# A WKV recurrence and a mixture of experts, one sequence apart, unrolled into one stage

## The chip, the cores and the metric

The kernel runs on one core of one Trainium2 chip. The metric is device microseconds, lower is better: the median of three runs, each of which is one execution of the whole program.

## The reference

Two blocks work on x, four sequences of 1024 tokens with 128 channels, f32. The first block (attention over whole sequences and six layers of local attention with feed-forward parts) is not touched. The second block is:

```python
h = _layernorm(x) * (1 + ca) + sa
x = x + ga * wkv(h)              # recurrence along each sequence
h = _layernorm(x) * (1 + cb) + sb
x = x + gb * mixture(h)          # per token, two of eight experts
# wkv:
r, v, k = split(h @ W_rvk.T)
#   per step: p = max(pp, u + k_t); e1 = exp(pp - p); e2 = exp(u + k_t - p)
#             y = (e1*aa + e2*v_t) / (e1*bb + e2)
#             p2 = max(pp + w, k_t); aa, bb, pp updated with exp(pp + w - p2), exp(k_t - p2)
out = (sigmoid(r) * y) @ W_out.T
# mixture:
probs = softmax(h @ gate_w.T); top2_w, top2_idx = top_k(probs, 2)
expert_out = silu(einsum(h, expert_w) + expert_b)      # all eight
out = sum(expert_out[top2_idx] * top2_w) @ combine_w.T
```

The recurrence needs its whole sequence in order, the mixture only its own tokens. So the mixture of sequence b needs the recurrence of sequence b and nothing of a later one.

## The kernel before

x stays in SBUF, transposed: 128 channels on the partitions, 4096 tokens along them. The program is a row of stages, each a block with its own instruction stream for every engine: `prepare`, `theta_attention`, `local_layers`, then `rwkv` and `mixture`. Between blocks all engines meet. Inside a block each engine has a queue that runs strictly in the order in which it is written, and waits on semaphores that other engines raise.

`rwkv` takes one sequence (1024 tokens) a step. TensorE makes k, v and r in three PSUM tiles of two banks each; ScalarE copies k and v, takes tanh of r (sr). VectorE makes pp, the running maximum, with a scan, then the arguments e1, e2, f1, f2 of four exponentials, which ScalarE takes. The denominators bb and the numerators aa are two more scans; then come den, its reciprocal, num, the output projection and the residual. GpSimd makes e2v and f2v. `step(n, late)` runs the recurrence of sequence `late` and puts the two layer norms of the next sequence n behind the arguments. A layer norm goes from engine to engine: mean on TensorE, centring on VectorE, squares on ScalarE, variances on TensorE, eleven small VectorE operations for 1/sqrt, a transpose that spreads it, the product on VectorE, the output on ScalarE.

`mixture` takes half a sequence (a chunk of 512 tokens) a step; there are eight. For each expert e TensorE multiplies (`ps_e`), ScalarE applies silu (`y`), GpSimd widens the gate (`wide`), TensorE transposes it (`ps_g`), VectorE multiplies both (`yg`, the function `gated`) and TensorE adds the product into the combined sum (`ps_c`). The layer norm, softmax and choice of the two best for the next chunk stand between the eight gatings. GpSimd widens one expert ahead. A chunk that is done is stored by the sync engine. exp and silu need different tables on ScalarE, so a switch between them has an ACT_TABLE_LOAD.

## Time and profile before

| | |
|---|---|
| Median of the three runs | 5023.8 us (5016.67 to 5025.26) |
| Profiled execution, its own time | 5043.72 us |
| Its span, first to last instruction | 5041.9 us |
| Mean granted TensorE clock | 0.945 |
| Recurrence stage, from 4588 us of the span | 234.0 us |
| Mixture stage, to the end of the span | 220.0 us |

The profile is of one execution. An engine's busy time is the time in which it executes; its waits are idle time in front of an instruction, put down to what ended them. The granted clock is 1.00 at TensorE's full speed (2.4 GHz) and 0.50 at half (1.2 GHz). In names from the profile, wkv_ stands for tiles of `rwkv` and moe_ for tiles of `mixture`. In a row of windows the busy times stand in the order TensorE matmul, TensorE weight load, VectorE, ScalarE, GpSimd, each with its number of instructions; then the clock, the DMA share and GB/s. An f32 matmul leaves two records.

### The profile page before, as it was taken

To read this page: it belongs to the slowest core of one execution; us is meant where nothing else is said; L and a number is where in the kernel's file an instruction comes from. 1 tells how busy PE (TensorE), PEld (TensorE's weight loads), DVE (VectorE), ACT (ScalarE), POOL (GpSimd) and SP (SyncE) were. 2 spreads that over 40 slices of the span, in tenths; PEclk is the share of its full clock that TensorE was granted. 3 is DMA by queue.
4 is the path that set the end of the run, shared out by engine and by line. 5 is a ranking of instruction groups with operands and counts; after the bars stand their busy time and mean duration, and the time that the engine had idled before them with its cause. 6 is when DMAs were issued, how large, how long until landed. Compare 5 with 4: busy or idle time off the path is not lost. (4 is left out here: it accounts for less than half of the span.)

```text
span 5041.9 us, 174816 instructions
## 1 busy us (share of the span) xinstructions
PE 4035.4 (80%) x68188; PEld 2875.6 (57%) x68188; DVE 3716.5 (74%) x6687; ACT 3142.5 (62%) x8425; POOL 1080.8 (21%) x856
## 2 busy tenths in 40 slices
PE   7948888888888888888888888888888888884358
PEld 4625665666666666666656665565666665652134
DVE  4837777777777777777777777777787787765655
ACT  4716666666776676776666666666666667661123
POOL 0002222222222222222222222222222222210011
PEclk9959999999999999999999999999999999996679
DMA  0012222222222222222222222222222222220000
GB/s 26 1 57 86 73 77 71 83 86 75 78 73 75 89 85 75 75 75 82 86 76 70 77 73 85 81 79 73 76 74 90 77 77 73 73 65 3 0 9 13
DMA packets 126159, 336.66 MB, mean 67 GB/s; under 512 B 32592, under 2 KB 33744, under 8 KB 125264
## 3 DMA queue, kind: packets, MB, share of 16 engines
q1 hardware_dynamic: 125520, 326.63, 20.1%
q8 instruction: 586, 9.60, 0.9%
q14 instruction: 53, 0.43, 0.0%
HBM read 22.41 MB, written 2.10 MB: 5 GB/s over the span
## 5 line engine op out<-in xcount | busy, mean ns | idle before, releaser
L1172 ACT ACTIVATE loc_probs<-loc_pair,loc_ebias,loc_rnorm 128x64 f32<-128x64 f32 x3072 | 1200.4, 432 | 11.6 <-DVE loc_ebias L1332 8.4
L873 POOL TENSOR_TENSOR loc_ks<-loc_mcos,loc_swapped 128x1024 f32<-128x1024 f32 x192 | 451.9, 2354 | 1771.7 <-DVE loc_kr L1320 1378.2
L920 PE MATMUL loc_pair<-loc_hs,loc_wqk 128*128 128x256 f32 x3072 | 750.8, 388 | 49.6 <-issue 45.3
L873 POOL TENSOR_TENSOR loc_qr<-loc_mcos,loc_swapped 128x1024 f32<-128x1024 f32 x192 | 452.1, 2355 | 1283.2 <-DMA loc_swapped<-loc_msin 1207.1
L1172 ACT ACTIVATION_READ_ACCUMULATOR loc_probs<-loc_pair,loc_ebias,loc_rnorm 128x1 f32 x3072 | 717.2, 233 | 0.0
L920 PEld LDWEIGHTS loc_pair<-loc_hs,loc_wqk 128*128 128x128 f32 x3072 | 568.3, 192 | 153.9 <-issue 66.3
L1330 DVE TENSOR_REDUCE loc_mx<-loc_pair 128x8 f32<-128x512 f32 x384 | 264.6, 689 | 413.7 <-PE loc_pair L964 399.0
L1272 DVE SCALAR_TENSOR_TENSOR loc_mcos<-loc_pair,loc_scal,loc_tab 128x1024 f32<-128x1024 f32 x384 | 490.5, 1277 | 85.1 <-ACT loc_sq L1154 66.7
L1154 ACT ACTIVATE loc_sq<-loc_pair 128x1024 f32<-128x1024 f32 x384 | 396.7, 1033 | 207.0 <-PE loc_pair L920 207.0
L1281 DVE SCALAR_TENSOR_TENSOR loc_msin<-loc_pair,loc_scal,loc_tab 128x1024 f32<-128x1024 f32 x384 | 489.7, 1275 | 9.1 <-DMA loc_swapped<-loc_msin 8.5
L964 PE MATMUL loc_pair<-loc_kr,loc_qr 64*32 64x64 f32 x24576 | 320.7, 225 | 126.7 <-issue 126.1
L977 PE MATMUL loc_pair<-loc_wv,loc_hs 128*64 128x512 f32 x1536 | 410.2, 659 | 1.6 <-DVE loc_o L1348 1.4
L1183 ACT ACTIVATE loc_vodd<-loc_pair 128x1024 f32<-128x1024 f32 x192 | 196.8, 1025 | 338.6 <-DMA loc_veven<-loc_vodd 206.0
L964 PEld LDWEIGHTS loc_pair<-loc_kr,loc_qr 64*32 64x32 f32 x24576 | 271.9, 105 | 226.8 <-issue 224.7
L1001 PE MATMUL loc_pair<-loc_veven,loc_probsT 64*32 64x64 f32 x12288 | 308.9, 226 | 84.9 <-issue 83.7
L1332 DVE SCALAR_TENSOR_TENSOR loc_ebias<-loc_mx,loc_rnorm 128x8 f32<-128x8 f32 x384 | 366.2, 954 | 13.2
L1190 ACT ACTIVATE loc_probsT<-loc_pair 128x1024 f32<-128x1024 f32 x192 | 195.8, 1020 | 275.9 <-PE loc_pair L986 275.9
L1197 ACT ACTIVATE loc_oT<-loc_pair 128x1024 f32<-128x1024 f32 x192 | 194.9, 1015 | 264.6 <-PE loc_pair L1011 264.6
L1021 PE MATMUL loc_one<-loc_oT,loc_wo 128*128 128x256 f32 x1536 | 347.6, 380 | 0.8 <-DVE loc_act_out L1393 0.4
L1001 PEld LDWEIGHTS loc_pair<-loc_veven,loc_probsT 64*32 64x32 f32 x12288 | 261.0, 105 | 148.5 <-issue 147.8
L1054 PE MATMUL loc_one<-loc_h,loc_w 128*128 128x256 f32 (+1 forms) x1152 | 322.6, 404 | 19.3 <-ACT loc_h L1211 8.1
L1001 PE MATMUL loc_pair<-loc_vodd,loc_probsT 64*32 64x64 f32 x12288 | 315.1, 227 | 5.0 <-issue 5.0
(240 smaller groups left out, 7440.5 us busy)
## 6 DMA issues: line engine op xcount, KB each, us to landing
loc_swapped<-loc_msin SPq DMA_DIRECT2D x768, 256.0 KB, 2.6
loc_veven<-loc_vodd SPq DMA_DIRECT2D x768, 64.0 KB
loc_veven<-loc_vodd SPq DMA_DIRECT2D x384, 128.0 KB
loc_wqk<-wqk_dram SPq DMA_DIRECT2D x12, 512.0 KB, 4.7
loc_wv<-wv_dram SPq DMA_DIRECT2D x6, 512.0 KB, 4.4
loc_wo<-wo_dram SPq DMA_DIRECT2D x6, 512.0 KB, 4.4
x<-xT_dram SPq DMA_DIRECT2D x1, 2048.0 KB, 7.3
loc_tab<-tables_dram SPq DMA_DIRECT2D x1, 2048.0 KB, 7.5
```

What stands on the lines that cost most here:

```text
L873: nc.gpsimd.tensor_tensor(dst, mcos[i % 2][:, :], swapped[:, :], ALU.add).then_inc(rope_add, 1)
L920: ins = nc.tensor.matmul(pairs[b][:, p // 2, (p % 2) * UNIT:(p % 2 + 1) * UNIT], wqk[:, k, w:w + P], hs[u.odd][:, :], start=True, stop=True)
L964: ins = nc.tensor.matmul(pairs[b][WIN * w:WIN * w + WIN, hp, p * 2 * WIN:(p + 1) * 2 * WIN], qr[u.odd][part, p, at:at + WIN], kr[u.odd][pa ...
L977: ins = nc.tensor.matmul(pairs[b][hp * DH:(hp + 1) * DH, g, :], hs[u.odd][:, BLK * x + DH * g:BLK * x + DH * g + DH], wv[:, hp, :], start= ...
L1001: ins = nc.tensor.matmul(pairs[b][WIN * w:WIN * w + WIN, hp, p * DH:(p + 1) * DH], probsT[part, p, WIN * w:WIN * w + WIN], v[part, w // 2, ...
L1021: ins = nc.tensor.matmul(bank(b)[:, 0:UNIT], wo[:, p, :], oT[:, p, :], start=p == 0, stop=p == PAIRS - 1)
L1054: ins = nc.tensor.matmul(bank(b)[0:FB[j], k * UNIT:(k + 1) * UNIT], w1[:, at:at + FB[j]], h[:, :], start=True, stop=True)
L1154: nc.scalar.activation(sq[:, i, :], flat(b), ACT.Square).then_inc(sq_ready, 1)
L1172: ins = nc.scalar.activation(probs[x][:, p, hp, :], pairs[b][:, hp, p * 2 * WIN:(p + 1) * 2 * WIN], ACT.Exp, bias=ebias[x][:, k:k + 1], sc ...
L1272: nc.vector.scalar_tensor_tensor(mcos[i % 2][:, :].rearrange("p (g t) -> p g t", g=4), flat(b).rearrange("p (g t) -> p g t", g=4), scal[u. ...
L1281: nc.vector.scalar_tensor_tensor(msin[:, :].rearrange("p (g t) -> p g t", g=4), flat(b).rearrange("p (g t) -> p g t", g=4), scal[u.odd][:, ...
L1332: nc.vector.scalar_tensor_tensor(ebias[x][:, k], mx[x][:, k], -1.0, rnorm[u.odd][:, x, HEADS:].rearrange("p (g y) -> p y g", y=2)[:, hp, : ...
```

## The change

`rwkv` and `mixture` become one block, `recurrence_and_mixture`, without loops. It is written out as stages: for each sequence b two halves (`part` 0 and 1). The first has the recurrence of b from the projections to the scan of the denominators, the second from the scan of the numerators to the residual, and the layer norms of sequence b+1. Beside them stand the eight experts of chunk `late` = n-1, and the norm and the choice of experts of chunk n = 2(b-1)+part. So the recurrence of sequence 0 has no mixture beside it, that of sequence 1 has chunk 0 in its second half, those of 2 and 3 have a chunk in each half, and three chunks are left after them.

To fit both into eight PSUM banks the recurrence has one bank (`ps_w`) for all projections: six matmuls of 512 tokens, each after ScalarE has emptied the bank, and an output projection in two halves, each after the other's residual. All layer norms share one set of buffers. The squares of a chunk's norm, before on VectorE, are taken on ScalarE. The weights of both parts are loaded at the start, and the first mean does not wait for them.

```diff
-def rwkv(nc, const, t):
+def recurrence_and_mixture(nc, const, t, out):
...
+        def both(stage):
+            for b in range(BATCH + 1):
+                for part in range(2):
+                    n = 2 * (b - 1) + part
+                    stage(part, b if b < BATCH else None, b + 1 if b + 1 < BATCH else None, n if n >= 0 else None, n - 1 if n >= 1 else None)
+            stage(0, None, None, None, NCH - 1)
...
+            def project(b, i):
+                if b is None:
+                    return
+                which, c = (2, 1, 0)[i // 2], i % 2
+                if i == 0:
+                    if b == 0:
+                        pe.wait_ge(wkv_loaded, START + 32)
+                    pe.wait_ge(ln.out_ready, START + norm_of_sequence(b, 1) + 1)
+                    pe.wait_ge(xw_done, START + 2 * b)
+                pe.wait_ge(proj_ready, START + 6 * b + i)
+                nc.tensor.matmul(ps_w[:, :], w[:, which, :], wh[:, half(c)], start=True, stop=True).then_inc(proj_ps, 1)
+            def project_out(b, c):
+                if b is None:
+                    return
+                pe.wait_ge(wy_ready, START + b + 1)
+                pe.wait_ge(proj_ready, START + 6 * b + 6)
+                pe.wait_ge(xw_done, START + 2 * b + c)
+                nc.tensor.matmul(ps_w[:, :], w[:, 3, :], num[:, half(c)], start=True, stop=True).then_inc(wout_ps, 1)
...
+                if part == 1:
+                    project_out(b, 0)
+                expert(late, 5)
+                combine(late, 4)
+                if part == 0:
+                    project(b, 5)
+                else:
+                    project_out(b, 1)
+                    if after_b is not None:
+                        mean(norm_of_sequence(after_b, 0), slice(after_b * SEQ, after_b * SEQ + CH))
+                expert(late, 6)
...
+            def times_values(b, i):
+                if b is None:
+                    return
+                pool.wait_ge(proj_ready, START + 6 * b + 4)
+                own_wait(pool, passed)
+                pool.wait_ge(wexp_ready, START + 4 * b + 2 * i + 2)
+                own_wait(pool, passed)
+                dst, src = ((e2v, e2), (f2v, f2))[i]
+                nc.gpsimd.tensor_tensor(dst[:, :], src[:, :], v[:, :], ALU.mult).then_inc(den_part, 1)
+            def stage(part, b, after_b, n, late):
+                for e in range(EXPERTS):
+                    widen(late, e)
+                    if part == 0 and e == 4:
+                        times_values(b, 0)
+                if part == 0:
+                    times_values(b, 1)
+            both(stage)
...
+            def stage(part, b, after_b, n, late):
                 if n is not None:
-
+                    if n == 0:
+                        act.wait_ge(moe_loaded, START + 80)
+                    ln.scalar_squares(act, norm_of_chunk(n))
+                silu(late, 0)
+                if part == 0:
+                    project_out(b, 0)
+                silu(late, 1)
+                if part == 0:
+                    project_out(b, 1)
+                if n is not None:
                     act.wait_ge(mods_ready, START + n + 1)
-                    for c in range(2):
-                        ln.scalar_squares(act, n * 2 + c)
-                        ln.scalar_out(act, n * 2 + c, [(slice(0, P), h[:, c * CH:(c + 1) * CH])], mods[:, 0:1])
-
-            sequences(act, step)
+                    ln.scalar_out(act, norm_of_chunk(n), [(slice(0, P), h[:, n % 2, :])], mods[:, n % 2, 0:1])
+                silu(late, 2)
+                if part == 0:
+                    project_out(b, 2)
+                silu(late, 3)
+                if part == 0:
+                    project_out(b, 3)
+                if n is not None:
+                    act.wait_ge(centred, START + n + 1)
+                    nc.scalar.activation(probs[:, :, :], logits[:, :, :], ACT.Exp).then_inc(exp_ready, 1)
+                if part == 0:
+                    exponential(b, 0)
+                    exponential(b, 1)
+                silu(late, 4)
+                silu(late, 5)
+                if part == 0:
+                    project_out(b, 4)
+                    project_out(b, 5)
+                    exponential(b, 2)
+                    exponential(b, 3)
+                elif after_b is not None:
+                    ln.scalar_squares(act, norm_of_sequence(after_b, 0))
+                silu(late, 6)
+                silu(late, 7)
+                if part == 1 and after_b is not None:
+                    sequence_out(after_b, 0)
+                    ln.scalar_squares(act, norm_of_sequence(after_b, 1))
+                    sequence_out(after_b, 1)
...
+            def first_part(b, n, late):
+                chunk_mods(n)
+                gated(late, 0)
+                if n is not None:
+                    rstd(norm_of_chunk(n))
+                gated(late, 1)
+                largest(b)
+                if n is not None:
+                    normed(norm_of_chunk(n), mods[:, n % 2, 1:2])
+                gated(late, 2)
+                arguments_state(b)
+                centred_logits(n)
+                gated(late, 3)
+                larger_now(b)
+                gated(late, 4)
+                arguments_now(b, 0)
+                softmax(n)
+                gated(late, 5)
+                arguments_now(b, 1)
+                two_best(n)
+                gated(late, 6)
+                denominators(b)
+                gated(late, 7)
+                chunk_done(late)
+            def second_part(b, after_b, n, late):
+                chunk_mods(n)
+                numerators(b)
+                gated(late, 0)
+                if n is not None:
+                    rstd(norm_of_chunk(n))
+                gated(late, 1)
+                denominators_now(b)
+                if n is not None:
+                    normed(norm_of_chunk(n), mods[:, n % 2, 1:2])
+                gated(late, 2)
+                reciprocals(b)
+                centred_logits(n)
+                gated(late, 3)
+                numerators_now(b)
+                received(b)
+                gated(late, 4)
+                softmax(n)
+                gated(late, 5)
+                if after_b is not None:
+                    sequence_mods(after_b)
+                residual(b, 0)
+                residual(b, 1)
+                if after_b is not None:
+                    centre(norm_of_sequence(after_b, 0), slice(after_b * SEQ, after_b * SEQ + CH))
+                two_best(n)
+                gated(late, 6)
+                if after_b is not None:
+                    rstd(norm_of_sequence(after_b, 0))
+                gated(late, 7)
+                if after_b is not None:
+                    normed(norm_of_sequence(after_b, 0), wmods[:, 1:2])
+                chunk_done(late)
+                if after_b is not None:
+                    sequence_norm(after_b, 1)
...
@@ -1808,9 +1996,7 @@
         if phases >= 2:
             local_layers(nc, const, t)
         if phases >= 3:
-            rwkv(nc, const, t)
-        if phases >= 4:
-            mixture(nc, const, t, out)
+            recurrence_and_mixture(nc, const, t, out)
         else:
             store(nc, const, out)
```

VectorE, in the second half of a recurrence, before (loop written out once for the last sequence): bb and aa are the scans, then den, its reciprocal and num.

```order
L1588 SCALAR_TENSOR_TENSOR wkv_bb<-wkv_e 128x1024
L1590 SCALAR_TENSOR_TENSOR wkv_aa<-wkv_e,wkv_e2v 128x1024
L1593 TENSOR_TENSOR wkv_den<-wkv_f,wkv_bb 128x1024
L1594 TENSOR_TENSOR wkv_den<-wkv_den,wkv_f 128x1024
L1595 RECIPROCAL wkv_den<-wkv_den 128x1024
L1596 TENSOR_TENSOR wkv_num<-wkv_f,wkv_aa 128x1024
L1598 TENSOR_TENSOR wkv_num<-wkv_num,wkv_f2v 128x1024
L1599 TENSOR_TENSOR wkv_num<-wkv_num,wkv_den 128x1024
```

The same place now, in a stage with a chunk beside it (tail_ names all tiles of the new block; yg is the gating of an expert; one and logits belong to the next chunk):

```order
L1767 TENSOR_TENSOR tail_yg<-tail_y,tail_ps_g 128x512
L1819 RECIPROCAL tail_den<-tail_den 128x1024
L1860 TENSOR_REDUCE tail_one<-tail_ps_small 128x4
L1861 TENSOR_TENSOR tail_logits<-tail_ps_small,tail_one 128x32
L1767 TENSOR_TENSOR tail_yg<-tail_y,tail_ps_g 128x512
L1824 TENSOR_TENSOR tail_num<-tail_f,tail_aa 128x1024
L1826 TENSOR_TENSOR tail_num<-tail_num,tail_f2v 128x1024
L1831 TENSOR_TENSOR tail_num<-tail_num,tail_den 128x1024
L1833 SCALAR_TENSOR_TENSOR tail_num<-tail_sr,tail_num 128x1024
L1767 TENSOR_TENSOR tail_yg<-tail_y,tail_ps_g 128x512
```

Between two gatings there is now the reciprocal and the centring of the logits, and between the next two all four products that end in num.

ScalarE, in the first half of a recurrence, before: the copy of v, tanh and four exponentials in one row.

```order
L1536 ACTIVATE wkv_v<-wkv_ps 128x1024
L1539 ACTIVATE wkv_sr<-wkv_ps 128x1024
L1542 ACTIVATE wkv_e<-wkv_e 128x1024 x2
L1542 ACTIVATE wkv_f<-wkv_f 128x1024 x2
```

The same place now (y0 and y1 are silu outputs of experts 3, 4 and 5; probs is the exponential for the gates):

```order
L1692 ACTIVATE tail_y<-tail_ps_e1,tail_expert_b 128x512
L1674 ACTIVATE tail_v<-tail_ps_w 128x512
L1722 ACT_TABLE_LOAD
L1722 ACTIVATE tail_probs<-tail_logits 128x32
L1684 ACTIVATE tail_e1<-tail_e1 128x1024
L1684 ACTIVATE tail_e2<-tail_e2 128x1024
L1692 ACT_TABLE_LOAD
L1692 ACTIVATE tail_y<-tail_ps_e0,tail_expert_b 128x512
L1692 ACTIVATE tail_y<-tail_ps_e1,tail_expert_b 128x512
L1677 ACTIVATE tail_sr<-tail_ps_w 128x512 x2
L1684 ACT_TABLE_LOAD
L1684 ACTIVATE tail_f1<-tail_f1 128x1024
```

The two silus of experts 4 and 5 stand behind three exponentials and two table loads, and tanh, which has no load of its own behind silu, stands behind them.

## Rows read from the trace of the kernel before

**Rows 1.** The page, part 1: busy us, share of the span, instructions.
```profile
PE 4035.4 (80%) x68188; PEld 2875.6 (57%) x68188; DVE 3716.5 (74%) x6687; ACT 3142.5 (62%) x8425; POOL 1080.8 (21%) x856
```

**Rows 2.** Windows, both stages: from:to, length, busy us by engine, clock, DMA.
```profile
4588.00:4822.00 234.00, 78.04 (x176) 38.96 (x176) 149.58 (x181) 40.07 (x46) 20.23 (x8) 0.57 0.00 1
4822.00:5042.00 220.00, 183.81 (x688) 100.44 (x688) 111.61 (x384) 72.62 (x97) 39.02 (x64) 0.91 0.04 13
```

**Rows 3.** Waits in the recurrence stage: total us, times, longest.
```profile
PE wkv_ps L1508 <- DVE wkv_num L1602: 88.5, 4, 28.9
...
DVE wkv_ln_var L194 <- PE wkv_ps_small L168: 21.0, 8, 2.7
...
PE wkv_ps_ln L162 <- DMA wkv_decay<-wkv_decay_dram: 16.3, 1, 16.3
```

**Rows 4.** Waits in the mixture stage.
```profile
DVE moe_yg L1737 <- ACT moe_y L1717: 49.3, 30, 2.9
```

**Rows 5.** Windows, one recurrence step: arguments, norms ahead, scans to num, output.
```profile
4669.30:4682.80 13.50, 6.25 (x14) 2.58 (x14) 10.49 (x7) 6.23 (x6) 2.34 (x1) 0.85 0.00 0
4682.80:4700.80 18.00, 8.04 (x26) 5.50 (x26) 6.84 (x30) 3.15 (x6) 2.35 (x1) 0.50 0.00 0
4700.80:4720.00 19.20, 0.23 (x1) 0.23 (x2) 18.28 (x9) 0.63 (x1) 0.00 (x0) 0.50 0.00 0
4720.00:4725.30 5.30, 3.71 (x5) 1.24 (x6) 1.44 (x2) 0.00 (x0) 0.00 (x0) 0.71 0.00 0
```

**Rows 6.** Windows, one mixture chunk beside the next one's norm; the last chunk.
```profile
4897.40:4922.00 24.60, 21.80 (x88) 11.86 (x87) 14.20 (x48) 8.90 (x12) 4.85 (x8) 1.00 0.03 11
5020.80:5038.60 17.80, 17.55 (x64) 8.81 (x63) 6.27 (x10) 5.50 (x8) 3.68 (x6) 1.00 0.04 15
```

**Rows 7.** Groups by line, VectorE in the recurrence stage: count, busy us, mean ns, idle before.
```profile
L1595 DVE RECIPROCAL wkv_den<-wkv_den 128x1024 f32<-128x1024 f32 x4 | 26.2, 6553 | 0.1
...
L1599 DVE TENSOR_TENSOR wkv_num<-wkv_num,wkv_den 128x1024 f32<-128x1024 f32 x4 | 4.9, 1226 | 0.1
```

**Rows 8.** Timeline, recurrence stage: start us, us, engine, line, idle before.
```profile
4591.44 2.08 PE L162 MATMUL wkv_ps_ln<-x,mean_w 128*128 128x512 f32 x2 [16.31 <-DMA wkv_decay<-wkv_decay_dram]
...
4596.92 0.16 DVE L194 TENSOR_SCALAR wkv_ln_var<-wkv_ps_small 128x4 f32<-128x4 f32 x1 [2.68 <-PE wkv_ps_small L168]
4597.12 0.17 DVE L91 TENSOR_SCALAR wkv_ln_rstd<-wkv_ln_var 128x4 int32<-128x4 int32 x1
...
4601.13 2.07 PE L162 MATMUL wkv_ps_ln<-x,mean_w 128*128 128x512 f32 x2 [0.84 <-DVE wkv_ln_normed L202]
...
4611.51 8.25 PE L1500 MATMUL wkv_ps<-wkv_h,wkv_w 128*128 128x512 f32 x12 [1.59 <-ACT wkv_h L222]
...
4669.34 5.39 PE L1500 MATMUL wkv_ps<-wkv_h,wkv_w 128*128 128x512 f32 x12 [1.59 <-DVE x L1605]
...
4676.04 2.19 ACT L1542 ACTIVATE wkv_e<-wkv_e 128x1024 f32<-128x1024 f32 x2 [0.24 <-DVE wkv_e L1570]
```

**Rows 9.** Timeline in a mixture chunk: ScalarE's table loads, exp and silu.
```profile
4910.25 1.28 ACT L1723 ACT_TABLE_LOAD   x1
...
4911.54 0.23 ACT L1723 ACTIVATE moe_probs<-moe_logits 128x32 f32<-128x32 f32 x1
4911.79 1.28 ACT L1717 ACT_TABLE_LOAD   x1
...
4913.09 1.46 ACT L1717 ACTIVATE moe_y<-moe_ps_e,moe_expert_b 128x512 f32<-128x512 f32 x2
```

**Rows 10.** Timeline, GpSimd's product e2v and VectorE's f1.
```profile
4678.31 2.34 POOL L1522 TENSOR_TENSOR wkv_e2v<-wkv_e,wkv_v 128x1024 f32<-128x1024 f32 x1 [47.91 <-ACT wkv_e L1542]
4678.37 3.35 DVE L1574 TENSOR_TENSOR wkv_f<-wkv_pp,wkv_pm 128x1024 f32<-128x1024 f32 x1
```

**Rows 11.** Windows of 1 us, as matmuls end and 3 us later.
```profile
4620.00:4621.00 1.00, 0.62 (x2) 0.00 (x0) 1.00 (x1) 1.00 (x2) 0.00 (x0) 1.00 0.00 0
4624.00:4625.00 1.00, 0.00 (x0) 0.00 (x0) 1.00 (x1) 0.68 (x1) 1.00 (x1) 0.54 0.00 0
```

More of the change, by code:

```diff
@@ L1693, in _ @@
+            for c in range(2):
+                ln.tensor(pe, c, x[:, half(c)], ps_ln[:, :], ps_small[:, 0:4])
+            both(stage)
         @block.gpsimd
         def _(pool):
[L1695 to L1703 removed]
@@ L1797, in kernel_program @@
+            sequence_mods(0)
+            for c in range(2):
+                sequence_norm(0, c)
+            dve.wait_ge(w_ready, START + 1)
+            link(nc.vector.tensor_scalar(wdec[:, :], ew[:, :], -1.0, None, ALU.mult))
+            dve.wait_ge(init, START + 1)
+            dve.wait_ge(wkv_loaded, START + 32)
+            dve.wait_ge(moe_loaded, START + 80)
+            both(stage)
 def kernel_program(nc, t, out, phases=5):
```

553 lines of the change are left out of this document (287 added, 266 removed).

## The prediction

> **What bounds the kernel now.** I read the page first: over the whole span TensorE is busy 80% and VectorE 74% [rows 1], but that is mostly the long local-attention part, which the change leaves alone. So I cut out the two stages that it touches. The recurrence stage is 234.0 us and the mixture stage 220.0 us, 454.0 together, a tenth of the span [rows 2]. In the first VectorE works 149.6 us, TensorE 78.0 at a mean granted clock of 0.57; in the second TensorE works 183.8 and VectorE 111.6 [rows 2]. So one is led by VectorE, the other by TensorE, and each leaves the other engine free for half its time: VectorE work adds up to 261.2 us of the 454.
>
> The chain of waits says how each is bound. In the recurrence TensorE waits 88.5 us for the last product num, and VectorE waits 21.0 for the variances [rows 3]: a serial chain. In the mixture VectorE waits 49.3 us for y [rows 4], while TensorE idles little. One recurrence step in windows [rows 5]: projections and arguments 13.5, the two layer norms of the sequence ahead 18.0 with VectorE at 6.8, scans to num 19.2 with VectorE at 18.3, output projection and residual 5.3. A mixture chunk is 24.6 us with VectorE at 14.2; the last one, with no chunk behind it, 17.8 [rows 6].
>
> **The change.** It removes no arithmetic. It puts the mixture of sequence b-1 into the VectorE, ScalarE, GpSimd and TensorE queues between the pieces of the recurrence of sequence b. What it adds: two more table loads; projections one bank at a time; residual in two halves (0.2 us a sequence). The squares of a mixture chunk move from VectorE (0.9) to ScalarE. Every queue runs in order, so the new time is VectorE's work plus the waits that its order leaves. I go through it by sequence.
>
> *Opening.* Before, the first mean starts at 4591.4, behind the weight transfers (TensorE's wait of 16.3 ends there), and the first projection at 4611.5, so 23.5 us from 4588 [rows 3, 8]. Now mean and centring start without that wait and only ScalarE's squares still need it: about 3 less, 20.5.
>
> *Sequence 0* has no mixture beside it. Arguments: 13.5 with half of its matmuls at the high clock [rows 5]; these are cold and go through one bank, each waiting for ScalarE's copy of the one before, so 17. Then 19.2 from the first scan to num [rows 5], of which the reciprocal is 6.55 [rows 7] (18.3 less it and less six products of 1.23 leaves 2.2 to 2.3 for each of the two scans); output in two halves, each waiting for the other's residual, 5.5; then the norms of sequence 1: 8.7 partly begun under the residual, and 9.6 (4601.13 less 4591.44 is 9.7 [rows 8]) with nothing beside it. In all 60, against 57.8 before (4611.5 to 4669.3 [rows 8]).
>
> *Sequence 2, the full case.* VectorE's work: recurrence 10.5 - 2.1 (a stall told below) + 18.3 + 1.4 + 0.2 = 28.3; norms of the next sequence 6.8 [rows 5]; two chunks of 14.2 less 0.9 for the squares, 26.6 [rows 6]. That is 61.7. Some 100 small operations follow each other 0.20 apart though each lasts 0.16 or 0.17 (4596.92, 4597.12 [rows 8]): 4 more, 65.7. Waits, walked in queue order with TensorE at 2.15 an expert (17.8 / 8 [rows 6]), silu 0.7, table load 1.28 [rows 9]:
> - centring waits for the mean in both halves, 1.3; the first gating for a silu behind the squares, 1.4; the variances, 0.5; the third gating of each half for a silu that now stands behind the norm's output on ScalarE, 2 x 1.45.
> - the fifth gating of the first half: on ScalarE its silu is behind load, exp of the gates, two exps of 1024 columns (2.19 for a pair [rows 8]), load: 1.28 + 0.23 + 2.2 + 1.28 + 0.7 = 5.7 after the v copies, where VectorE has only 1.8 of work: 3.8. The seventh gating behind tanh, load, two exps, load: 1.0.
> - end of chunk 0.5; residual of the second half 0.9; second norm of the next sequence, exposed behind the last gating, 3.2.
>
> Waits 15.5, so 81. To this I add 4 for the clock: TensorE stands still under the reciprocal and the products behind it, and a stretch without matmuls lets the clock fall (1.00 in 4620 to 4621 as the matmuls end, 0.54 in 4624 to 4625 [rows 11]); what is cold then is one output projection, two experts and the mean. And 3 for the port, below. 88.
>
> *Sequence 1* is without the eight gatings in its first half: 72 + 3 + 2 = 77. *Sequence 3* is without the next norms and their wait: 72 + 4 + 3 = 79. *After the last recurrence* two chunks as now, 49.2, and the last with the store, 17.8 + 3.2 = 21.0.
>
> Sum: 20.5 + 60 + 77 + 88 + 79 + 49 + 21 = 394.5, against 454: **60 us less**. The profiled execution took 5043.7 us for its span of 5041.9; the median of the runs is 5023.8, 20 below it. The part that differs is the same in both, so I take 60 off the median: 4964.
>
> **The port.** While GpSimd's product e2v runs from 4678.31 for 2.34, VectorE's f1, begun at 4678.37, takes 3.35 where a 1024-column product alone takes 1.23 [rows 7, 10]. It stood still for 2.1, until GpSimd was done. The new stage has 40 gate copies of 0.61 on GpSimd beside sequences 1 to 3, where they used to run beside gatings that read PSUM. If each costs VectorE nothing it is 0; if each hits a product of SBUF operands at its start, 40 x 0.6 = 24. Most copies start as TensorE ends a transpose, at random against VectorE, which is in such products a third of the time: I take 8.
> The Trainium skill, "SBUF — State Buffer", section "Who interferes with whom", says that a VectorE instruction with two SBUF inputs and a GpSimd instruction that reads SBUF exclude each other for the whole of the one begun first. By that, the trace agrees, and the loss to VectorE is capped at the copy's own length.
>
> **Table loads.** From 4910.25 a load of 1.28, exp at 4911.54, the next load at 4911.79, silu at 4913.09 [rows 9]: a switch costs 1.28 and no more. The Trainium skill, "ScalarE: Activation LUTs", section "What ACT_TABLE_LOAD costs", has about 2.66 us for a switch, drain included. By it the fifth and seventh gating of sequences 2 and 3 would come 4 to 5 later each time and the sum would be about 9 higher, 4973. The row decides here.
>
> **The rivals.**
> - *Nothing but VectorE's work counts* in sequences 1 to 3. For: VectorE's pieces are long enough to cover most round trips. Against: the waits above are by order, not by speed. Work is 66 + 59 + 58 = 183 against 244, 61 more, so 4903 at the bound; half of it, 4934. Chance 8%.
> - *TensorE stays at the low clock* through sequences 1 to 3. For: the recurrence stage has 0.57 [rows 2] and the gaps in it stay. Against: the mixture stage has 0.91, and chunks put work on TensorE every 3 us. Its work in sequence 2 is two chunks of 21.8 [rows 6], eight projections of 0.9 (six take 5.39 [rows 8]) and two norms of 2 (8.0 at the low clock, [rows 5]), 54.8 at the high clock and 109 at the low: 21 over my 88, 30 with a few waits kept. Sequence 3 is two chunks and the projections, 50.8 and 101, 22 over; sequence 1, with one chunk, 73, 0 to 8 over. In all 43 to 60 more, 5014 in the middle. Chance 9%.
> - *The queues lock*: every in-order engine waits at another's piece, and a stage is the sum of its parts: 56 + 49 for sequence 2 (17 over), 15 over for each other, so 47 and 5011. For: ScalarE's queue now has both chains. Chance 6%.
> - *Slower, by the port.* If a copy that meets a scan of 2.3 us waits for it, TensorE's transposes wait for the copy, and the gating for them, each of the 40 costs the 2.1 that the product in [rows 10] lost: 84 us, 5048. It decides from 1.5 us a copy (60 / 40). Against: the copies run one expert ahead. Chance 4%.
>
> **The numbers.** My forecast has 73%. The own range of the forecast: waits and adders 15 off either way, 4949 to 4979. To leave out no more than 2 in 10 I reach to the half-way case below and into the cold-clock case above: 4938 to 5006. A measurement of this kernel tells 0.2%, 10 us, from no change (the three runs spread over 8.6). Faster by more: the forecast, the first rival, half of the second and of the third (below 5014), 0.89. Within: the other halves, 0.07. Slower: 0.04.
>
> **What would show it.** In the changed profile the combined stage lasts 380 to 410 us; VectorE is busy 250 to 270 us of it; sequence 2 takes 82 to 94 us and is the longest. The longest wait of VectorE on ScalarE stands before the fifth gating (the line of yg), 3 to 5 us, twice. The reciprocal has mixture work of TensorE and ScalarE under it. Granted clock 0.8 to 0.95 in sequences 2 and 3, 0.5 in sequence 0. The local layers are unchanged. Wrong would be: a clock near 0.5 beside the mixture, products of VectorE with a mean far above 1.5 us, or gatings that wait 2 us nearly every time.

## The result, and the profile after

The changed kernel took 4974.65 us in the median of four runs (4962.77 to 4999.60), the kernel before 5024.53 beside it. The ratio is 0.9906, 95% interval 0.9881 to 0.9930. A second set of five runs gave 4972.76 and 0.9896 (0.9878 to 0.9915). The forecast was 4964.

Single runs of one kernel lie up to 43 us apart (5009.73 to 5052.84 for the kernel before, in the last set), so the profiles are compared by their **tail**: the time from the end of VectorE's last update of x in the local layers, which the change leaves alone, to the end of the span. That update in the kernel before (timeline; start, duration, eight instructions):

```profile
4576.19 10.35 DVE L1444 SCALAR_TENSOR_TENSOR x<-loc_xa,mod,x 64x1024 f32<-64x1024 f32 x8
```

It ends at 4586.54, and the span at 5041.9: a tail of 455.4. The same row and the span in the changed kernel:

```profile
4569.25 10.34 DVE L1444 SCALAR_TENSOR_TENSOR x<-loc_xa,mod,x 64x1024 f32<-64x1024 f32 x8
```

```profile
core 0: 4983.1 us, clock 0.950
```

It ends at 4579.59, so the tail is 403.5, **51.9 us shorter**. The other 6.9 of the 58.8 between the two spans lie in the untouched layers. Over all kernels measured here their end varies from 4551 to 4592. The page's part 1, to set against [rows 1]:

```profile
PE 4053.0 (81%) x68188; PEld 2876.0 (58%) x68188; DVE 3701.7 (74%) x6683; ACT 3147.4 (63%) x8447; POOL 1095.9 (22%) x856
```

The shares hardly move, since the tail is a twelfth of the span. Windows by sequence of the new stage (columns as in [rows 2]). The second begins at the first projection, the later ones where VectorE starts on the next stage's factors of the norm:

```profile
4579.90:4602.90 23.00, 10.14 (x29) 6.05 (x29) 6.89 (x30) 4.05 (x6) 0.14 (x3) 0.50 0.15 39
4602.90:4662.60 59.70, 25.44 (x44) 9.29 (x44) 38.80 (x45) 9.34 (x13) 7.33 (x2) 0.53 0.00 0
4662.60:4741.90 79.30, 55.63 (x152) 27.98 (x152) 57.18 (x132) 22.12 (x31) 14.27 (x12) 0.69 0.01 4
4741.90:4834.30 92.40, 66.83 (x216) 34.34 (x216) 61.24 (x142) 31.26 (x42) 19.55 (x18) 0.83 0.02 6
4834.30:4915.90 81.60, 63.65 (x191) 31.67 (x192) 54.13 (x113) 29.39 (x39) 19.57 (x18) 0.83 0.01 4
4915.90:4983.10 67.20, 60.03 (x235) 31.88 (x233) 32.30 (x103) 24.34 (x34) 13.38 (x22) 0.99 0.05 17
```

These are the opening, sequences 0 to 3, and the chunks left over. VectorE is busy 250.5 us of 403. Sequence 2 is the longest, and there VectorE works 61.2 of 92.4. The clock rises from 0.53 with no mixture beside the recurrence to 0.83 with a chunk in each half. What VectorE waits for in the tail (total us, times, longest):

```profile
DVE tail_yg L1767 <- ACT tail_y L1692: 56.3, 32, 4.6
DVE tail_ln_var L194 <- PE tail_ps_small L168: 20.7, 10, 5.1
```

The wait for num that held TensorE for 88.5 us [rows 3] has shrunk to 31.3, of which 20.9 are one wait, that of sequence 0. The dearest wait of VectorE is the one for y, 56.3 us, where it was 49.3 in the mixture alone [rows 4]. Groups by line in the tail:

```profile
L1637 POOL COPY tail_wide<-tail_gates 128x512 f32<-128x512 f32 x64 | 51.4, 813 | 189.7 <-PE tail_ps_g L1550 189.7
...
L1819 DVE RECIPROCAL tail_den<-tail_den 128x1024 f32<-128x1024 f32 x4 | 26.2, 6546 | 0.0
...
L1801 DVE TENSOR_TENSOR_SCAN tail_bb<-tail_e 128x1024 f32<-128x1024 f32 x4 | 11.9, 2974 | 0.1
```

GpSimd's gate copies have a mean of 813 ns, where a copy alone takes 610. The reciprocal is unchanged from [rows 7]. The scan bb has a mean of 2974 ns where a scan alone takes 2290.

### The profile page after: what moved, and what is told of

Its sections match the earlier page's. It is cut to its first block and busy times, and to the rows that moved or that the text cites. A ratio compares the mean times of both kernels' runs of the same rounds, so it can differ in the third digit from the quotient of the medians.

```text
span 4983.1 us, 174228 instructions
## 1 busy us (share of the span) xinstructions
PE 4053.0 (81%) x68188; PEld 2876.0 (58%) x68188; DVE 3701.7 (74%) x6683; ACT 3147.4 (63%) x8447; POOL 1095.9 (22%) x856
## 3 DMA queue, kind: packets, MB, share of 16 engines
q1 hardware_dynamic: 125520, 326.63, 20.4%
## 5 line engine op out<-in xcount | busy, mean ns | idle before, releaser
L1332 DVE SCALAR_TENSOR_TENSOR loc_ebias<-loc_mx,loc_rnorm 128x8 f32<-128x8 f32 x384 | 379.8, 989 | 13.2
```

What stands on the lines that cost most here:

```text
L1332: nc.vector.scalar_tensor_tensor(ebias[x][:, k], mx[x][:, k], -1.0, rnorm[u.odd][:, x, HEADS:].rearrange("p (g y) -> p y g", y=2)[:, hp, : ...
```

## The experiments

Each kernel differs from the changed one by the edit shown; the code is cut. e4_narrow_copy and e11_narrow_values also set their tiles to zero once, and e1_serial numbers the layer norms in its own order. e2, e3, e4 and e11 leave out or replace part of the computation; the others compute all of it. A time is one run where no number stands beside it, and each tail is read from one profile.

| kernel | its time, us | tail, us | to 403.5 |
|---|---|---|---|
| changed, second set | 4972.76 (5 runs) | 404.2 | +0.7 |
| e1_serial | 5029.79 | 451.9 | +48.4 |
| e2_one_table | 4955.29 | 393.4 | -10.1 |
| e3_short_recip | 4931.85 | 378.6 | -24.9 |
| e4_narrow_copy | 4955.33 | 399.1 | -4.4 |
| e5_silu_first | 4979.24 | 398.1 | -5.4 |
| e6_regroup | 4986.88 | 393.0 | -10.5 |
| e7_filler | 4974.95 | 399.4 | -4.1 |
| e8_split_reciprocal | 4987.67 | 404.0 | +0.4 |
| e9_all_three | 4958.69 (6 runs) | 384.1 | -19.4 |
| e11_narrow_values | 4964.37 | 387.0 | -16.5 |
| e12_values_on_vector | 4955.74 (5 runs) | 387.1 | -16.4 |

**How far a tail can be trusted.** The changed kernel once more, unedited.

> The changed kernel once more, unedited, for more runs of it beside those of the kernel before and of the version with three edits. Its tail should be 403.5 within 1 us while its whole time differs from the first profile's by up to 30 us, if what varies between runs lies in the local layers ahead of the tail. Rival: the tail varies as well, by some 3 us or more, and then differences of 4 us in the other runs mean nothing.

Its profile has a span 12.2 us shorter and a tail 0.7 us longer. So what varies lies mostly ahead of the tail, and a difference of 4 us between tails is read here as one of the kernels. The 0.7 lies in sequence 0 (60.6 for 59.8); sequences 1 to 3 and the chunks left agree within 0.1 us in the two profiles (79.3, 92.3, 81.7 and 67.1). All this rests on two profiles of the same kernel.

**Merging without overlap.**

```diff
-            for b in range(BATCH + 1):
+            for b in range(BATCH):
                 for part in range(2):
-                    n = 2 * (b - 1) + part
-                    stage(part, b if b < BATCH else None, ...)
+                    stage(part, b, b + 1 if b + 1 < BATCH else None, None, None)
+            for n in range(NCH):
+                stage(n % 2, None, None, n, n - 1 if n >= 1 else None)
```

> The same single unrolled block, but all four recurrences first and the eight chunks after them, nothing side by side. I read the tail: from the end of VectorE's last update of x in the local layers to the end of the span (455.4 us before, 403.5 in the changed kernel). My theory, that the overlap is the gain: about 450 (the pause of 7.6 us between the two blocks goes and the opening is 1.5 shorter; one bank for the projections gives some 3 back in a sequence). Rival, that one block without loops and branches is itself the gain: 405 to 425.

The tail is 451.9, 3.5 under the kernel before. Of the 51.9 us, 48.4 come from the overlap and 3.5 from everything else that the rewriting did. VectorE's largest wait in this kernel (total us, times, longest):

```profile
DVE tail_yg L1768 <- ACT tail_y L1693: 60.9, 43, 2.9
```

The wait for y is 60.9 us without overlap and 56.3 with it. The overlap hides mixture work inside the recurrence; it does not shorten the mixture's own round trip.

**Table loads.**

```diff
-nc.scalar.activation(y[...], ps_e[...], ACT.Silu, bias=...)
+nc.scalar.activation(y[...], ps_e[...], ACT.Tanh, bias=...)
```

> silu of the experts is replaced by tanh, which stands in one table with exp, so that no table is loaded in the stage after the first (part of the computation is changed). Tail 403.5 in the changed kernel. My theory, that the fifth and seventh gating wait for silus behind two table loads each: about 386, with the waits before these gatings down from 4.6 and 3.9 us to 2 or less each. Rival, that VectorE's work hides the loads: 400 or more.

Nineteen loads of 1.28 us are gone, 24.4 us of ScalarE, and the tail is 10.1 shorter, a little over half of what the theory had. Sequence 1 keeps its 79.3; the gain is 4.2 in sequence 2, 3.5 in sequence 3 and 2.3 in the chunks left. The longest wait for y is now 2.1:

```profile
DVE tail_yg L1767 <- ACT tail_y L1692: 39.0, 29, 2.1
```

In sequence 2 the fifth gating waits 1.79 and the seventh 1.95, where they waited 4.64 and 3.92. So a load counts only where a gating waits for it: of the 24.4 us, 10.1 came out of the tail. The Trainium skill, "ScalarE: Activation LUTs", section "What ACT_TABLE_LOAD costs", has 1283 ns for the load and some 1380 more for a drain; the first part agrees with the rows, the second is not seen: in the timeline of sequence 2 below, a load of 1.28 begins at 4775.78 and silu at 4777.07.

**Is VectorE's queue the bound?**

```diff
-link(nc.vector.reciprocal(den[:, :], den[:, :]))
+link(nc.vector.tensor_tensor(den[:, :], den[:, :], f2[:, :], ALU.mult))
```

> The reciprocal of den (6.55 us) is replaced by a product with f2 (1.23 us), which changes part of the computation. Tail 403.5 in the changed kernel; in the kernel before the same edit could give at most 4 x 5.3 = 21. My theory, that VectorE's queue sets the time but experts run under the reciprocal: all of 5.3 in sequence 0 and 3.5 in each of the others, so about 387. Rival, that TensorE or ScalarE set the time beside the mixture: 5 to 8 in all, 396 or more.

VectorE has 4 x 5.33 = 21.3 us less work, and the tail is 24.9 shorter, where the theory had some 16: the whole of the work came out, and 3.6 besides. By sequence the gain is 5.7, 8.2, 6.9 and 4.0. Sequence 2 of this kernel takes 85.4, 7 less than the 92.4 above for 5.3 less work, at a clock of 0.86, where it was 0.83 (in sequence 1 0.79, where it was 0.69):

```profile
4699.70:4785.10 85.40, 64.49 (x216) 33.59 (x216) 56.24 (x142) 31.25 (x42) 20.10 (x18) 0.86 0.02 7
```

That the higher clock gives the 3.6 would fit, but no run shows it.

Cutting the same reciprocal in two halves, with a gating between them:

```diff
-                reciprocals(b)
+                reciprocals(b, 0)
                 centred_logits(n)
                 gated(late, 3)
+                reciprocals(b, 1)
```

> The reciprocal of 1024 columns (6.54 us) is made in two halves of 512, and the centring of the logits and the fourth gating stand between the halves instead of behind both. The full computation is made. Tail of the changed kernel: 403.5 us. Theory: what the reciprocal costs is its time on VectorE, and VectorE's queue sets the end, so an order alone gives back no more than TensorE's idle time under it is worth: tail 401 to 406. Rival: the single block of 6.5 us hurts by its length, since TensorE, ScalarE and GpSimd run dry and the clock falls; cut in two it costs 2 to 3 us less in each of sequences 1 to 3: tail 394 to 398.

The tail is 404.0. It is the time on VectorE that costs, not the length of the block.

**GpSimd's gate copies.**

```diff
-nc.gpsimd.tensor_copy(wide[:, e % 2, :, :], bcast_last(gates[...], P))
+nc.gpsimd.tensor_copy(wide[:, e % 2, :, 0:8], bcast_last(gates[...], 8))
```

> GpSimd widens each gate to 8 columns instead of 128 (the rest of the tile stays zero, so part of the work is left out); its 64 copies are much shorter. Tail 403.5 in the changed kernel. My theory, that the shared port costs little through these copies: 400 to 403. Rival, that the copies block VectorE's products beside the mixture: 385 to 395.

4.4 us for 64 copies whose time on GpSimd falls from 51.4 to 20.4, a little more than the theory's 0.5 to 3.5; 3.6 of it is in sequences 1 to 3, the rest in the chunks left. What the remaining 20.4 us of copies cost no run shows. That settles the rival "slower, by the port": it needed 1.5 us a copy.

**GpSimd's products with the values.**

```diff
-nc.gpsimd.tensor_tensor(dst[:, :], src[:, :], v[:, :], ALU.mult)
+nc.gpsimd.tensor_tensor(dst[:, 0:8], src[:, 0:8], v[:, 0:8], ALU.mult)
```

> GpSimd's two products with the values are made on the first 8 of their 1024 columns, the rest is zero, so the recurrence's numerator is changed. Tail of the changed kernel: 403.5 us. Theory: VectorE's scan bb and product den of sequence 0 (4.44 and 3.18 us, where other sequences show 2.29 and 1.22) and its f2 and scan aa of sequence 1 (3.31 and 3.15, where others show 1.28 and 2.29) are longer because GpSimd's product runs beside them; they fall to the short values, 7 us less: tail 395 to 398. Rival: they are long for another reason, or the time goes into waits: tail 402 to 404.

16.5 us, over twice what was expected. The four places named did fall to their short values, and VectorE's busy time fell by 8.0 (250.5 to 242.5). The scan bb, by its group:

```profile
L1803 DVE TENSOR_TENSOR_SCAN tail_bb<-tail_e 128x1024 f32<-128x1024 f32 x4 | 9.2, 2288 | 0.1
```

The other half is in waits. By sequence the gain is 3.3, 6.1, 3.7 and 3.3, and VectorE's busy time fell by 4.1, 2.8, 0.5 and 0.6 of it: the waits are in sequences 1 to 3. Sequence 2 of the changed kernel, timeline from the load behind e1 and e2 to the seventh gating (4777.79):

```profile
4764.17 1.28 ACT L1692 ACT_TABLE_LOAD   x1
4764.34 2.34 POOL L1647 TENSOR_TENSOR tail_e2v<-tail_e,tail_v 128x1024 f32<-128x1024 f32 x1 [9.67 <-ACT tail_e L1684]
...
4766.24 0.69 DVE L1767 TENSOR_TENSOR tail_yg<-tail_y,tail_ps_g 128x512 f32<-128x512 f32 x1 [4.64 <-ACT tail_y L1692]
4766.62 2.72 POOL L1637 COPY tail_wide<-tail_gates 128x512 f32<-128x512 f32 x3
...
4767.28 1.11 PE L1550 MATMUL tail_ps_g<-ident,tail_wide 128*128 128x128 f32 x4 [3.32 <-POOL tail_wide L1637]
...
4769.90 1.92 PE L1530 MATMUL tail_ps_w<-tail_wh,tail_w 128*128 128x512 f32 x2
...
4771.85 0.60 ACT L1677 ACTIVATE tail_sr<-tail_ps_w 128x512 f32<-128x512 f32 x1 [4.63 <-PE tail_ps_w L1530]
...
4773.76 2.00 ACT L1684 ACTIVATE tail_f<-tail_f 128x1024 f32<-128x1024 f32 x2
...
4775.78 1.28 ACT L1692 ACT_TABLE_LOAD   x1
...
4777.07 1.26 ACT L1692 ACTIVATE tail_y<-tail_ps_e,tail_expert_b 128x512 f32<-128x512 f32 x2
4777.79 0.69 DVE L1767 TENSOR_TENSOR tail_yg<-tail_y,tail_ps_g 128x512 f32<-128x512 f32 x1 [3.92 <-ACT tail_y L1692]
```

Read it from POOL's row at 4764.34. While GpSimd makes e2v, the copy of the next gates stands behind it, so TensorE waits 3.32 us for it at 4767.28. Then TensorE is at the low clock: the last projection at 4769.90 takes 1.92 for its two records. ScalarE's tanh waits 4.63 for that projection, the load and the exponentials stand behind the tanh, and the seventh gating waits 3.92 us. In the kernel with narrow products the same place is:

```profile
4751.15 0.66 PE L1550 MATMUL tail_ps_g<-ident,tail_wide 128*128 128x128 f32 x4 [1.19 <-POOL tail_wide L1639]
...
4753.95 1.02 PE L1530 MATMUL tail_ps_w<-tail_wh,tail_w 128*128 128x512 f32 x2
```

TensorE waits 1.19, the projection takes 1.02, and the seventh gating waits 1.45:

```profile
4761.09 0.69 DVE L1769 TENSOR_TENSOR tail_yg<-tail_y,tail_ps_g 128x512 f32<-128x512 f32 x1 [1.45 <-ACT tail_y L1694]
```

**Two orders.** The silu of expert 2 ahead of the norm's output:

```diff
+                silu(late, 2)
                 if n is not None:
                     act.wait_ge(mods_ready, START + n + 1)
                     ln.scalar_out(act, norm_of_chunk(n), ...)
-                silu(late, 2)
```

> One change on ScalarE: in every chunk the silu of expert 2 stands ahead of the output of the chunk's layer norm, no longer behind it. The full computation is made. Tail is the time from the end of VectorE's last update of x in the local layers to the end of the span: 403.5 us in the changed kernel. Theory: VectorE's queue sets the time and its third gating waits 1.42 us for that silu in each of the halves with a chunk behind it (seen at 4704.69, 4756.47, 4797.10), seven halves in all; the norm's output then comes 0.7 later, which centring of the logits has slack for because TensorE and the scans lie between. Tail 393 to 397. Rival: the norm's output is as urgent as the silu (TensorE waits 2.02 us for it at 4796.55), so the wait moves to the logits and the expert behind them: tail 401 to 406.

5.4, between the two theories. By sequence the gain is 1.3, 1.8 and 3.0, and the chunks left are 0.7 longer: there the third gating still waits 0.82 and the centring of the logits, which had no wait, waits 1.0 in each of two chunks, as the rival had it. In the second halves of sequences 1 to 3 the wait of 1.42 is simply gone. In the first half of sequence 2 it moves on: the fourth gating, which had no wait, has one of 1.50, the fifth waits 6.25 instead of 4.64, the seventh 1.76 instead of 3.92. Rows of sequence 2 (TensorE's wait for the copy behind e2v, the last projection, fifth and seventh gating), then the same but for the fifth in sequence 3 of the same profile:

```profile
4766.92 0.69 DVE L1767 TENSOR_TENSOR tail_yg<-tail_y,tail_ps_g 128x512 f32<-128x512 f32 x1 [6.25 <-ACT tail_y L1692]
...
4767.97 0.66 PE L1550 MATMUL tail_ps_g<-ident,tail_wide 128*128 128x128 f32 x4 [3.33 <-POOL tail_wide L1637]
...
4769.32 1.02 PE L1530 MATMUL tail_ps_w<-tail_wh,tail_w 128*128 128x512 f32 x2
...
4776.32 0.69 DVE L1767 TENSOR_TENSOR tail_yg<-tail_y,tail_ps_g 128x512 f32<-128x512 f32 x1 [1.76 <-ACT tail_y L1692]
```

```profile
4855.94 1.12 PE L1550 MATMUL tail_ps_g<-ident,tail_wide 128*128 128x128 f32 x4 [3.33 <-POOL tail_wide L1637]
...
4858.56 1.91 PE L1530 MATMUL tail_ps_w<-tail_wh,tail_w 128*128 128x512 f32 x2
...
4866.45 0.69 DVE L1767 TENSOR_TENSOR tail_yg<-tail_y,tail_ps_g 128x512 f32<-128x512 f32 x1 [3.92 <-ACT tail_y L1692]
```

These rows part what the section on GpSimd's products left together. TensorE waits 3.33 us for the copy behind e2v in both sequences, as it waited 3.32 in the changed kernel. In sequence 2 the granted clock stays at 1.00 behind the wait, the projection takes 1.02 and the seventh gating waits 1.76. In sequence 3 it falls (0.50), the projection takes 1.91 and the seventh gating waits 3.92. So of the 3.92 some 2.2 us are the low clock; the late copy costs by letting it fall. Why the clock fell behind one of two equal waits no run shows.

The exponentials of the first half in one group:

```diff
+                silu(late, 4)
                 ...
-                    exponential(b, 0)
-                    exponential(b, 1)
-                silu(late, 4)
+                    for i in range(4):
+                        exponential(b, i)
                 silu(late, 5)
                 ...
-                    exponential(b, 2)
-                    exponential(b, 3)
```

and on VectorE both arguments ahead of the fifth gating.

> The first half of each sequence's stage in another order. ScalarE: silu of expert 4, then the exponential of the gates and all four exponentials of the recurrence together, one table load back, silu of expert 5, the two tanh; so two switches of the table where there were four. VectorE: both arguments f1 and f2 stand ahead of the fifth gating instead of behind the fifth and sixth. The full computation is made. Tail of the changed kernel: 403.5 us. Theory: the waits before the fifth and seventh gating of the first half (4.64 and 3.92 us in sequence 2) come of ScalarE's chain of loads and exponentials and not of VectorE's work; one of the two goes, and 2 or 3 us are spent before the sixth gating instead. Gain 2 to 3 us in each of sequences 2 and 3: tail 396 to 400. Rival: the chain is only put together, and the sixth gating waits for what the fifth and seventh waited for: tail 402 to 407.

10.5, more than the theory had. Timeline of sequence 2 in this kernel:

```profile
4770.94 1.28 ACT L1723 ACT_TABLE_LOAD   x1
...
4776.27 1.28 ACT L1692 ACT_TABLE_LOAD   x1
...
4778.72 0.69 DVE L1765 TENSOR_TENSOR tail_yg<-tail_y,tail_ps_g 128x512 f32<-128x512 f32 x1 [0.23 <-PE tail_ps_g L1550]
...
4783.91 0.69 DVE L1765 TENSOR_TENSOR tail_yg<-tail_y,tail_ps_g 128x512 f32<-128x512 f32 x1 [4.50 <-ACT tail_y L1692]
```

The first half has two loads where it had four (16 in the tail for 20), 4770.94 and 4776.27. The fifth gating no longer waits, the sixth waits 0.23, and only the seventh waits long, 4.50. ScalarE's order and VectorE's were changed together, so what each is worth is not shown. It also helps sequence 1, whose stage from the first projection to the next is 78.4 instead of 81.6. That part was not foreseen, and no run takes it apart either.

**The clock under the reciprocal.**

```diff
+            def filler(b, count):
+                pe.wait_ge(proj_ready, START + 6 * b + 6)
+                for i in range(count):
+                    nc.tensor.matmul(ps_w[:, :], w[:, 3, :], w[:, :, :], start=True, stop=True)
```

> Seven products of 128x512 whose result nobody uses are given to TensorE in the second half of each sequence's stage: three ahead of the fourth combine and four ahead of the output projection, where it stands idle for 2.5 and 3.8 us while VectorE makes the reciprocal and the products behind it. The full computation is made besides. Tail of the changed kernel: 403.5 us. Theory of the clock term (4 us a sequence in the prediction): the granted clock falls to 0.50 there (4808 to 4814) because TensorE stands idle, so that the output projection takes 2.08 and the next expert 1.91 us, where they take 1.10 and 1.02 at the high clock; with the fillers they run at the high clock and VectorE's waits for the residual and the fifth gating shrink. By these rows 3 us in each of sequences 1 to 3: tail 393 to 397, and the clock in the 12 us behind the reciprocal over 0.9. Rival: those waits are not on VectorE's path, or the fillers push back the work behind them: tail 401 to 407 with the clock at 0.9 or more all the same.

In the changed kernel the place looks so (window behind the reciprocal, up to num; timeline of the output projection, the next expert and the sixth gating, which the expectation miscounts as the fifth):

```profile
4805.20:4810.20 5.00, 1.13 (x2) 0.30 (x2) 4.90 (x6) 1.75 (x2) 0.00 (x0) 0.72 0.00 0
```

```profile
4810.26 2.08 PE L1538 MATMUL tail_ps_w<-tail_num,tail_w 128*128 128x512 f32 x2 [3.78 <-DVE tail_num L1833]
...
4812.13 1.91 PE L1547 MATMUL tail_ps_e<-tail_h,tail_expert_w 128*128 128x512 f32 x2
...
4814.80 0.69 DVE L1767 TENSOR_TENSOR tail_yg<-tail_y,tail_ps_g 128x512 f32<-128x512 f32 x1 [2.20 <-ACT tail_y L1692]
```

TensorE is busy 1.13 of 5.0 us, the clock falls, and the projection takes 2.08. With the fillers:

```profile
4798.00:4803.00 5.00, 4.65 (x11) 1.91 (x12) 4.90 (x5) 1.44 (x2) 0.00 (x0) 1.00 0.00 0
```

```profile
4798.80 3.60 PE L1543 MATMUL tail_ps_w<-tail_w 128*128 128x512 f32 x8
4802.75 1.12 PE L1538 MATMUL tail_ps_w<-tail_num,tail_w 128*128 128x512 f32 x2 [0.35 <-DVE tail_num L1842]
4803.71 1.02 PE L1552 MATMUL tail_ps_e<-tail_h,tail_expert_w 128*128 128x512 f32 x2
```

The clock is 1.00, the projection takes 1.12 and the expert 1.02, and the sixth gating waits 0.41 where it waited 2.20:

```profile
4805.49 0.69 DVE L1776 TENSOR_TENSOR tail_yg<-tail_y,tail_ps_g 128x512 f32<-128x512 f32 x1 [0.41 <-ACT tail_y L1701]
```

The tail fell by 4.1: from first projection to first projection 1.6 in sequence 1 and 1.7 in sequence 2, and 0.7 behind them. The mechanism is shown, at less than half the price that I gave this place.

**All three together.**

> The three edits together: silu of expert 2 ahead of the norm's output, the first half's exponentials in one group, and the seven fillers on TensorE. The full computation is made. By themselves they took 5.4, 10.5 and 4.1 us off the changed kernel's tail of 403.5. Theory, that VectorE's queue sets the time: they remove different waits and add up, 20 less: tail 382 to 386, and the median 20 below that of the changed kernel, ratio to it 0.996. Rival, that they free the same waits (the first put its gain of the first half into the fifth gating, which rose to 6.25 us, and that is the wait of the second): 11 to 15 less, tail 388 to 393, ratio 0.9975.

The tail is 384.1, 19.4 less, where the three single gains add up to 20.0. Sequence 2, the seventh gating of the first half, the third and sixth of the second:

```profile
4750.15 0.69 DVE L1774 TENSOR_TENSOR tail_yg<-tail_y,tail_ps_g 128x512 f32<-128x512 f32 x1 [4.46 <-ACT tail_y L1701]
...
4766.27 0.68 DVE L1774 TENSOR_TENSOR tail_yg<-tail_y,tail_ps_g 128x512 f32<-128x512 f32 x1
...
4782.86 0.69 DVE L1774 TENSOR_TENSOR tail_yg<-tail_y,tail_ps_g 128x512 f32<-128x512 f32 x1 [1.10 <-ACT tail_y L1701]
```

Of the waits of 4.64 and 3.92 one of 4.46 is left, the third gating no longer waits, and the 2.20 of the second half is 1.10. This version computes everything the reference does. Its median was 4958.69 in six runs, beside 4972.76 for the changed kernel in five; to the kernel before the ratio is 0.9874 (0.9850 to 0.9897). The intervals of the two versions overlap, so the whole times do not tell the 14 us between the medians from nothing with certainty; the tails do.

**Giving the products back to VectorE**, in the version with three edits:

```diff
+                dst, src = ((e2v, e2), (f2v, f2))[i]
+                link(nc.vector.tensor_tensor(dst[:, :], src[:, :], v[:, :], ALU.mult))
+                dve.sem_inc(den_part, 1)
```

> The version with three edits, and GpSimd's two products with the values made by VectorE instead: e2v right ahead of the scan aa, f2v right ahead of the sum that reads it. GpSimd keeps only the gate copies. The full computation is made. The tail of the version with three edits is 384.1 us. Eight products of 1.22 us more on VectorE are 9.8. Theory: GpSimd's products cost 16.5 us of the tail when they are there (measured by narrowing them), 8.0 of it in longer VectorE instructions and 8.5 in waits for gate copies that queue behind them, so the move gives 6.7 back: tail 376 to 380. Rival: the waits were already taken away by the new order of the exponentials (the seventh gating waits no more), so only the 8.0 comes back against 9.8 spent: tail 384 to 388.

The tail is 387.1, 3.0 more than without the move and in the rival's range, but not for its reason. VectorE is busy 252.8 us of the tail instead of 252.4: with 9.8 us of work added, its other instructions are 9.4 shorter, not 8.0: mainly the scans bb and aa (11.3 to 9.1 and 11.1 to 9.9) and the small operations that make the gates (the cast 4.2 to 1.5, the two comparisons behind it 6.5 to 3.0). What is left, 2.6, is in waits, and 1.5 of it in the chunks left, where neither kernel has such a product. No run shows where it comes from, and 3.0 between two single profiles is less than the 4 us that are read here as a difference. So the move is worth nothing that these runs can tell. That the new order of the exponentials had already taken the waits was not shown by itself. The ratio to before is 0.9854 (0.9824 to 0.9884), not to be told from 0.9874.

## Why the prediction was right, and where it was off

The direction and the cause held, and the size within a seventh: the tail fell by 51.9 for a forecast of 60. Cut as the prediction cut it (from 1.46 us behind the last local update, as 4588 was), in us:

| part | predicted | measured | difference |
|---|---|---|---|
| opening | 20.5 | 21.8 | +1.3 |
| sequence 0 | 60 | 59.8 | -0.2 |
| sequence 1 | 77 | 79.3 | +2.3 |
| sequence 2 | 88 | 92.3 | +4.3 |
| sequence 3 | 79 | 81.7 | +2.7 |
| chunks left, store | 70 | 67.2 | -2.8 |
| sum | 394.5 | 402.1 | +7.6 |

- **VectorE's work plus the waits of its order** is the right model. e1 gives 48.4 of 51.9 to the overlap, and e3 gives back every microsecond taken from VectorE's queue. The signs named ahead came as well: a stage of 402 us, VectorE busy 250, 92 for sequence 2, a clock of 0.83 in sequences 2 and 3.
- **Part of the closeness is luck.** In sequence 2 VectorE's work, the gaps between small operations and the port were put at 61.7 + 4 + 3 = 68.7; measured are 61.2 busy and 2.4 in gaps too short for the list of waits, 63.6. The waits and the clock were put at 15.5 + 4 = 19.5; the waits listed add up to 28.8. One side was 5.1 too high and the other 9.3 too low, and only the difference shows in the table.
- **Fifth gating of the first half**: 3.8 predicted (the terms given, 5.7 less 1.8, make 3.9), 4.64 measured, in sequences 2 and 3 both. The chain of load, exponentials and load is the one told; e2 and e6 move it.
- **Seventh gating: "1.0 by tanh, load, two exps, load"**: 3.92 in sequence 2 and 3.90 in sequence 3. This is the term that was mis-sized most, twice. The walk through the queues left out GpSimd's: the copy of the gates stands behind e2v, TensorE behind the copy, and what follows runs at the low clock. With narrow products it is 1.45; with whole products and the clock high it is 1.76 (e5, sequence 2).
- **Third gating**: 2 x 1.45 predicted, 1.42 in each half. Exact, and e5 shows that it came from the order alone. Seven such waits are 9.9 us; taking them away was worth 5.4, since 1.1 came back in sequence 2 and 3.5 in the chunks left.
- **End of the chunk**: 0.5 predicted, 2.17 measured. The last combine starts at 4781.76 at the low clock and takes 2.08. The first centring waits 2.12 for its mean, where 1.3 was set down for both halves.
- **The clock, 3 to 4 a sequence**: at the place that the prediction named it is 0.7 to 1.7. A second place, behind e2v, was not named and costs some 2.2 in sequence 2 by the rows of e5, so there the two make 3.9: about the right sum, half of it in the wrong place. The last combine and the first mean, both at the low clock too, were not measured by themselves.
- **The port, 8 for 40 gate copies**: narrowing all 64 is worth 4.4, and 3.6 of it in sequences 1 to 3. The loss through the products is larger, but not new: VectorE's f1, f2 and scan aa took 6.4 + 2.1 + 2.0 us above their plain durations in the kernel before, by their groups' busy times (11.3 to 4.9, 7.2 to 5.1, 11.1 to 9.1), and 8.0 is what narrowing took off VectorE in the changed one.
- **Table loads by the row, not by the longer figure**: right, though the sum by the longer figure, 4973, lies nearer to the measured 4974.65 and 4972.76 than the forecast. That is chance: load and silu still follow each other 1.29 us apart (4775.78, 4777.07), and what was missing stands in the bullets above.
- **The rivals.** Nothing but work counts: no, there are 56.3 us of waits for y. The low clock through sequences 1 to 3: no, 0.69, 0.83 and 0.83. The queues lock: in small, before the fifth and seventh gating, 8.6 us of waits where 4.8 were put down; sequence 2 came out 4.3 over the forecast, not 17. Slower by the port: no, by e4.

## What to carry to other kernels

When two chains are woven into in-order queues, walk every queue that a buffer passes, the helper engine's as well: the wait that was missed here began on GpSimd, went through TensorE, whose clock fell with it, and ScalarE, and showed on VectorE under ScalarE's name. Then count how often ScalarE changes its table in a round, and put the exponentials together; that, one more change of order and fillers on TensorE took another 19 us off the stage with the same computation. Work put on a helper engine is not free even when the engine is idle: compare its price in locks and in queueing with the price of doing it at home, which in the last experiment came out about even.

## What the runs showed of the hardware

**The port locks scans too, and both ways.** Timeline, sequence 0 of the changed kernel:

```profile
4615.90 3.12 POOL L1647 TENSOR_TENSOR tail_e2v<-tail_e,tail_v 128x1024 f32<-128x1024 f32 x1 [35.86 <-ACT tail_e L1684]
...
4616.73 4.44 DVE L1801 TENSOR_TENSOR_SCAN tail_bb<-tail_e 128x1024 f32<-128x1024 f32 x1
...
4621.42 4.21 POOL L1647 TENSOR_TENSOR tail_f2v<-tail_f,tail_v 128x1024 f32<-128x1024 f32 x1 [2.40 <-ACT tail_f L1684]
4623.53 3.18 DVE L1813 TENSOR_TENSOR tail_den<-tail_f,tail_bb 128x1024 f32<-128x1024 f32 x1
```

GpSimd's e2v begins while VectorE is in f2 (4615.53 to 4616.81) and takes 3.12 instead of 2.34. The scan bb begins under it and takes 4.44 instead of 2.29; its excess of 2.15 is about what was left of e2v (4619.02 less 4616.73 is 2.29). Then f2v begins in the scan aa and takes 4.21, and den, begun under f2v, takes 3.18 instead of 1.22. With the products narrow all scans take 2.29. The Trainium skill, "SBUF — State Buffer", section "Who interferes with whom", has the rule for VectorE instructions with two SBUF inputs; these rows agree, and show it for the scan.

**Run to run, the noise sits in one place.** Between two profiles of the same program the untouched local layers ended 12.9 us apart and the tails differed by 0.7. For a change confined to a stage, the stage's own length shows a much smaller change than the whole time can.
